# The tail of a ViT-tower kernel on one core: values, turns, scales and stores reordered, and two groups' outputs moved from VectorE to ScalarE and GpSimd

## The reference

```
lu, ru, ld, rd = four copies of x shifted by 4 pixels diagonally
c = concat(x, lu, ru, ld, rd)                    # 10 channels
c = (c - mean(c)) * rsqrt(var(c) + 1e-7) * gamma + beta    # per image
h = conv(c, W, stride 8) + b                     # 13 x 13 = 169 tokens of 128
h = concat(cls_tok, h)
n = layernorm(h);  q, k, v = n Wq^T, n Wk^T, n Wv^T
for t in tokens:  S = S + 0.01 * sum_b v[b,t] k[b,t]^T;  out[:, t] = S q[:, t]
h = h + out
result = h + ffn(layernorm(h))
```

## Time and profile before

| | |
|---|---|
| median of three runs | 229.32 us |
| the profiled execution | 229.03 us |
| its span | 227.2 us |
| TensorE busy | 198.8 us, 87% |
| GpSimd busy | 157.6 us, 69% |
| VectorE busy | 154.2 us, 68% |
| ScalarE busy | 112.1 us, 49% |
| granted TensorE clock, mean | 0.974 |

### The profile page before, as it was taken

One profiled execution on the slowest core, in us unless ns is written; L12 is line 12 of the kernel. 1 busy time (PEld: TensorE's weight loads), 2 busy tenths in 40 slices (PEclk: granted clock), 3 DMA queues, 4 the chain that ended last, 5 costly groups with the idle time before them and its releaser, 6 DMA issues.

```text
span 227.2 us, 4909 instructions
## 1 busy us (share of the span) xinstructions
PE 198.8 (87%) x1558; PEld 169.3 (75%) x1558; DVE 154.2 (68%) x760; ACT 112.1 (49%) x244; POOL 157.6 (69%) x124
## 2 busy tenths in 40 slices
PE   0299997899899999999999999999999999988500
PEld 0289886677688899888888888899888888876300
DVE  2658983351576786687777768579649866976971
ACT  6002211345334555565656585575566558475642
POOL 1049869899982899968999579669999235253130
PEclk9999999999999999999999999999999999999955
DMA  6999957913113005162053602012101211201434
GB/s 171 369 426 421 423 239 113 372 75 82 77 17 143 3 0 179 34 191 58 3 165 83 185 23 46 22 28 49 46 3 46 48 27 24 46 4 46 109 79 100
DMA packets 16543, 26.00 MB, mean 114 GB/s; under 512 B 1319, under 2 KB 13277, under 8 KB 16262
## 3 DMA queue, kind: packets, MB, share of 16 engines
q1 hardware_dynamic: 15836, 25.18, 34.7%
q10 hardware_dynamic: 682, 0.51, 0.7%
HBM read 19.77 MB, written 5.92 MB: 113 GB/s over the span
## 4 chain that ended last, share of the span: by engine, by line
PE 64%; DMA 12%; POOL 9%; DVE 8%; issue 2%; ACT 2%; SPq 0%; DVEq 0%; ACTq 0%; POOLq 0%
PE conv L462 29%; DMA rows<-x_windows 12%; PE vr_ps L504 11%; PE first_ps L514 9%; PE outs L531 9%; POOL scaled L382 7%; PE turn L494 4%; DVE scaled L382 2%; PE conv L468 2%; DVE images L819 1%; DVE state L790 1%; DVE state L798 1%; POOL g_low L1091 1%; DVE ln_stats L824 1%; PE conv L504 1%
## 5 line engine op out<-in xcount | busy, mean ns | idle before, releaser
L462 PE MATMUL conv<-scaled,wt 128*128 128x256 f32 (+3 forms) x460 | 116.0, 372 | 9.9 <-DMA wt<-weight 9.9
L382 POOL TENSOR_TENSOR scaled<-rows,gam 128x832 f32<-128x832 f32 x60 | 93.8, 1586 | 6.2 <-PE conv L462 4.2
L462 PEld LDWEIGHTS conv<-scaled,wt 128*128 128x128 f32 x460 | 77.1, 193 | 18.0 <-DMA wt<-weight 9.9
L666 ACT ACTIVATE values<-vr_ps,rstd 128x256 f32<-128x256 f32 x78 | 37.0, 475 | 64.8 <-PE vr_ps L504 54.5
L1101 POOL TENSOR_TENSOR rstd<-var,powers 128x8 f32<-128x8 f32 (+2 forms) x20 | 30.4, 1518 | 23.9 <-DVE var L810 23.9
L790 DVE TENSOR_TENSOR state<-first_ps,state 128x128 f32<-128x128 f32 x80 | 23.3, 291 | 31.5 <-PE first_ps L514 26.8
L674 ACT ACTIVATE images<-images,ln_shift,ln_gain 128x128 f32<-128x128 f32 x82 | 37.9, 484 | 4.8 <-DVE ln_shift L858 4.8
L504 PE MATMUL vr_ps<-w_high,g_low 128*128 128x256 f32 x80 | 32.0, 400 | 0.4 <-ACT values L666 0.4
L1091 POOL TENSOR_TENSOR g_low<-g_t,g_high 128x512 fp32r<-128x512 f32 x21 | 26.8, 1274 | 6.7 <-ACT g_high L653 5.9
L779 DVE BATCH_NORM_STATS2 ln_stats<-images 128x6 f32<-128x128 f32 x85 | 23.7, 284 | 6.7 <-ACT images L660 6.6
L798 DVE TENSOR_TENSOR state<-second_ps,state 128x128 f32<-128x128 f32 x80 | 22.6, 282 | 2.1 <-issue 0.3
(11 more groups left out here) (147 smaller groups left out, 236.6 us busy)
## 6 DMA issues: line engine op xcount, KB each, us to landing
rows<-x_windows SPq DMA_DIRECT2D x13, 864.0 KB, 5.6
out<-images SPq DMA_DIRECT2D x41, 128.0 KB, 2.4
images<-x_rows SPq DMA_DIRECT2D x3, 624.0 KB, 21.8
images<-x_rows SPq DMA_DIRECT2D x1, 1456.0 KB, 13.0
images<-x_rows SPq DMA_DIRECT2D x1, 1248.0 KB, 15.5
images<-x_rows SPq DMA_DIRECT2D x1, 832.0 KB, 19.6
small<-smalls SPq DMA_DIRECT2D x1, 512.0 KB, 8.6
terms<-parked SPq DMA_DIRECT2D x3, 168.0 KB
```

The lines of the kernel that those rows point to most:

```text
L382: return eng.tensor_tensor(scaled[:, s, at:at + N], window, gains, ALU.mult)
L462: last = pe.matmul(conv_ps[g % 2][:, at:at + n * B], wt[:, s], scaled[:, s, a % RING:a % RING + n], start=first, stop=(g < EARLY and s == ...
L666: act.activation(values[:, t % VALUE_SLOTS].rearrange("p a e -> p (a e)"), vr_bank(t)[:, 0:2 * E], ACT.Identity, scale=rho_of(t)).then_inc ...
```

## The change

- TensorE: `turn(LAST)` moves from the start of the tail into step 71, before `vr(75)`. `vr(82)` and `vr(83)` move ahead of `reads(18)`.
- ScalarE: `rows_out(20)` ahead of `values_out(76)`, `high(20)` behind it; finishing of tile 57 leaves step 70 and comes into the tail. New `out_copy(t)` for tiles 72 to 79: the output bank times rho into `h2`, laid between finished tiles.
- GpSimd: new `add_outs(g)` for groups 18 and 19: `h2 = h2 + h`, one 128x512 `tensor_tensor`.
- VectorE: `add_out` of tiles 72 to 79 goes; statistics of the tail's tiles are laid anew; `ln2_stats_of` of tiles 72 to 79 waits for GpSimd's sum. `ln2_affine(19)` comes before `ln2_moments(20)`.
- SyncE: tile 84 and the first half of group 20 leave in one DMA, behind the same waits.

```diff
@@ SyncE
-            sp.wait_ge(result_ready, LAST + 1)
-            sp.dma_start(out[:, PATCHES], tile_of(result, OUT_SLOTS, TILES - 1)[0:B]).then_inc(last_stored, 16)
             sp.wait_ge(result_ready, LAST + 2)
             sp.wait_ge(last_three_ready, 1)
-            sp.dma_start(out[:, bass.ds(1 + TOKENS * LAST, PER_GROUP, 2)],
-                         result[LAST % OUT_SLOTS].rearrange("p (k e) -> p k e", e=E)[0:B]).then_inc(last_stored, 16)
+            at = (H_SLOTS + H2_SLOTS + LAST % OUT_SLOTS) * width
+            sp.dma_start(out[:, bass.ds(1 + TOKENS * LAST, PER_GROUP + 1, 2)],
+                         spare[0:B, at:at + (PER_GROUP + 1) * E].rearrange("p (k e) -> p k e", e=E)).then_inc(last_stored, 16)
@@ TensorE, step
+                if t == TAIL - 1:
+                    turn(LAST)
                 if t + PER_GROUP >= 0:
                     vr(t + PER_GROUP)
@@ TensorE, tail
-                turn(LAST)
                 turn(LAST + 1)
...
                 vr(TAIL + 9)
+                vr(TAIL + 10)
+                vr(TAIL + 11)
                 pe.wait_ge(h2_ready, tile_no(TAIL - 1))
                 reads(g)
-                vr(TAIL + 10)
-                vr(TAIL + 11)
                 vr(TAIL + 12)
@@ ScalarE
+            def out_copy(t):
+                g, at = t // PER_GROUP, (t % PER_GROUP) * E
+                act.wait_ge(out_done, tile_no(tiles_of(g)[-1]))
+                act.activation(tile_of(h2, H2_SLOTS, t), out_bank(g)[:, at:at + E], ACT.Identity,
+                               scale=rho_of(t)).then_inc(out_scaled, 1)
...
-                    if finish_step(k) == t < TAIL - 1:
+                    if finish_step(k) == t < TAIL - 2:
                         finish_next(k)
@@ ScalarE, tail
+                rows_out(LAST)
                 values_out(TAIL + 4)
-                rows_out(LAST)
+                high(LAST)
                 rows_out(LAST + 1)
                 values_out(TAIL + 5)
-                high(LAST)
                 values_out(TAIL + 6)
                 values_out(TAIL + 7)
                 high(LAST + 1)
-                for t in range(TAIL - 14, TAIL - 11):
+                for t in range(TAIL - 15, TAIL - 11):
                     finish_next(t)
                 for t in LAST_TILES:
                     values_out(t)
-                for t in range(TAIL - 11, TAIL - 8):
+                finish_next(TAIL - 11)
+                for t in range(TAIL, TAIL + 4):
+                    out_copy(t)
+                for t in range(TAIL - 10, TAIL - 8):
                     finish_next(t)
+                for t in range(TAIL + 4, TAIL + 8):
+                    out_copy(t)
                 for t in range(TAIL - 8, LAST_TILES[0]):
                     finish_next(t)
@@ VectorE
             def ln2_stats_of(t):
-                dve.wait_ge(h2_ready, tile_no(t))
+                if TAIL <= t < LAST_TILES[0]:
+                    dve.wait_ge(pool_h2_ready, t // PER_GROUP - TAIL // PER_GROUP + 1)
+                else:
+                    dve.wait_ge(h2_ready, tile_no(t if t < TAIL else t - 2 * PER_GROUP))
@@ VectorE, tail, from the states of group 20 on
                 first_state(LAST_TILES[0])
-                add_out(TAIL)
                 second_state(LAST_TILES[0])
-                add_out(TAIL + 1)
                 first_state(LAST_TILES[1])
-                add_out(TAIL + 2)
                 second_state(LAST_TILES[1])
-                add_out(TAIL + 3)
+                ln2_affine(g - 1)
                 first_state(LAST_TILES[2])
-                ln2_affine(g - 1)
+                ln2_stats_of(TAIL)
                 second_state(LAST_TILES[2])
-                ln2_stats_of(TAIL)
+                ln2_stats_of(TAIL + 1)
                 first_state(LAST_TILES[3])
-                ln2_stats_of(TAIL + 1)
+                ln2_stats_of(TAIL + 2)
                 second_state(LAST_TILES[3])
-                ln2_stats_of(TAIL + 2)
+                ln2_stats_of(TAIL + 3)
                 first_state(LAST_TILES[4])
-                ln2_stats_of(TAIL + 3)
                 ln2_moments(g)
                 ln2_variance(g)
-                for t in tiles_of(g + 1):
+                group_stats(g + 1)
+                for t in LAST_TILES:
                     add_out(t)
-                group_stats(g + 1)
                 ln2_affine(g)
                 ln2_moments(g + 1)
                 ln2_variance(g + 1)
                 for t in LAST_TILES:
-                    add_out(t)
-                for t in LAST_TILES:
                     ln2_stats_of(t)
+                ln2_affine(g + 1)
                 ln2_moments(LAST)
                 ln2_variance(LAST)
-                ln2_affine(g + 1)
                 ln2_affine(LAST)
@@ GpSimd
+            def add_outs(g):
+
+                pool.wait_ge(out_scaled, tiles_of(g)[-1] - TAIL + 1)
+                pool.tensor_tensor(h2[g % H2_SLOTS], h2[g % H2_SLOTS], h[g % H_SLOTS], ALU.add).then_inc(pool_h2_ready, 1)
@@ GpSimd, tail
                 ln2_power(LAST - 3)
+                add_outs(TAIL // PER_GROUP)
+                add_outs(TAIL // PER_GROUP + 1)
                 ln2_power(LAST - 2)
```

More of the change, by code:

```diff
@@ L300, in tower @@
         last_three_ready = sem("last_three_ready")
+        out_scaled = sem("out_scaled")
+        pool_h2_ready = sem("pool_h2_ready")
         last_stored = sem("last_stored")
@@ L451, in _ @@
             sp.wait_ge(cls_stored, 16)
-            sp.wait_ge(last_stored, 48)
+            sp.wait_ge(last_stored, 32)
         @block.tensor
@@ L907, in tail @@
                 ln2_affine(g - 3)
+                ln1_stats_of(LAST_TILES[0])
                 first_state(TAIL)
-                ln1_stats_of(LAST_TILES[0])
+                ln1_stats_of(LAST_TILES[1])
                 second_state(TAIL)
-                ln1_stats_of(LAST_TILES[1])
+                ln1_stats_of(LAST_TILES[2])
                 first_state(TAIL + 1)
-                ln1_stats_of(LAST_TILES[2])
+                ln1_stats_of(LAST_TILES[3])
                 second_state(TAIL + 1)
-                ln1_stats_of(LAST_TILES[3])
+                ln1_stats_of(LAST_TILES[4])
                 first_state(TAIL + 2)
-                ln1_stats_of(LAST_TILES[4])
+                ln2_affine(g - 2)
                 second_state(TAIL + 2)
@@ L921, in tail @@
                 ln1_variance(LAST_TILES, last_var[:])
+                add_out(TAIL - 4)
                 second_state(TAIL + 3)
-                ln2_affine(g - 2)
-                add_out(TAIL - 4)
+                add_out(TAIL - 3)
                 first_state(TAIL + 4)
-                add_out(TAIL - 3)
+                add_out(TAIL - 2)
                 second_state(TAIL + 4)
-                add_out(TAIL - 2)
+                add_out(TAIL - 1)
                 first_state(TAIL + 5)
-                add_out(TAIL - 1)
+                ln2_stats_of(TAIL - 4)
                 second_state(TAIL + 5)
-                ln2_stats_of(TAIL - 4)
+                ln2_stats_of(TAIL - 3)
                 first_state(TAIL + 6)
-                ln2_stats_of(TAIL - 3)
+                ln2_stats_of(TAIL - 2)
                 second_state(TAIL + 6)
-                ln2_stats_of(TAIL - 2)
+                ln2_stats_of(TAIL - 1)
                 first_state(TAIL + 7)
-                ln2_stats_of(TAIL - 1)
+                ln2_moments(g - 1)
                 second_state(TAIL + 7)
-                ln2_moments(g - 1)
                 ln2_variance(g - 1)
                 first_state(LAST_TILES[0])
-                add_out(TAIL)
                 second_state(LAST_TILES[0])
-                add_out(TAIL + 1)
                 first_state(LAST_TILES[1])
-                add_out(TAIL + 2)
                 second_state(LAST_TILES[1])
-                add_out(TAIL + 3)
+                ln2_affine(g - 1)
                 first_state(LAST_TILES[2])
-                ln2_affine(g - 1)
+                ln2_stats_of(TAIL)
                 second_state(LAST_TILES[2])
-                ln2_stats_of(TAIL)
+                ln2_stats_of(TAIL + 1)
                 first_state(LAST_TILES[3])
-                ln2_stats_of(TAIL + 1)
+                ln2_stats_of(TAIL + 2)
                 second_state(LAST_TILES[3])
-                ln2_stats_of(TAIL + 2)
+                ln2_stats_of(TAIL + 3)
                 first_state(LAST_TILES[4])
-                ln2_stats_of(TAIL + 3)
                 ln2_moments(g)
                 ln2_variance(g)
-                for t in tiles_of(g + 1):
+                group_stats(g + 1)
+                for t in LAST_TILES:
                     add_out(t)
-                group_stats(g + 1)
                 ln2_affine(g)
```

## The result

| | us | ratio to before, 95% |
|---|---|---|
| before, median of 6 | 229.27 | |
| after, median of 6 | 227.38 | 0.992 (0.9909 to 0.993) |
| forecast | 227.1 (226.3 to 228.2) | |
| lowest of the versions tried (e10) | 226.21 | 0.9866 (0.9851 to 0.9881) |

The change gains 1.89; 2.25 was forecast. The mechanism is the forecast's up to the last issue; the landing behind it is not. The profiled execution took 227.42 with a span of 225.6. Ahead of every edit this trace already lies 0.27 later than the one of before (ScalarE's values(73) at 195.78 against 195.51), so 0.27 has to be taken off its positions when they are compared; behind the edits of part 1 it lies only 0.17 later (values at 201.16 against 200.99), which is what part 1 gains. The number in brackets is the position in the kernel before, as it stands.

What follows compares the result with a forecast made beforehand. VectorE was taken to set when the final store stream begins, and its bytes to decide the end. Work moved off VectorE and earlier products start the stream 2.25 earlier: 229.32 - 2.25 = 227.1, range 226.3 to 228.2.

Steps and rivals of the forecast that it cites:

- Bound: End of the kernel: set by when the final store stream begins, which VectorE's work sets; stream needs at least 2.8.
- Part 1: Group 20's transposes a step early, ScalarE's work ahead, finish tiles shifted: taken as 0, bounds -0.2 to +0.25.
- Part 2: vr(82), vr(83) ahead of reads(18) on TensorE: VectorE's first state of group 20 at 209.59 in place of 210.25.
- Rival E: Part 2 brings no earlier products; their gain is mostly eaten by the stall anyway: 227.3; chance 0.60 together with the forecast.
- Part 3: Outputs of groups 18 and 19 off VectorE: var(20) at 218.51 against 220.07, scale of group 19 2.25 earlier.
- the stall: VectorE's new wait of 0.42 for GpSimd at the statistics of tile 72, behind first_state(82).
- Rivals C and D: C: ScalarE and GpSimd hand over late, 227.7 or 227.9, chance 0.17. D: GpSimd's adds long enough to decide, 0.09.
- Part 4: Final stores: last issue 2.96 earlier, but the 544 KB stream ends at 223.95 against 226.2 and decides: 2.25.
- The prediction's own sign of being wrong: End of the kernel: forecast wrong if the last landing lay further than 3.2 behind the last issue.
- Rival B: The bytes don't bind; the end follows SyncE's last issue, 2.96 earlier: 226.4; chance 0.14.
- The rule weighed in part 3: GpSimd about 2x slower than VectorE on two-input elementwise work; by it 2.1 per group and about 227.9.

Runs made afterwards that it cites:

- e10: e7 with the second half of group 19's store issued by GpSimd in place of SyncE; 226.21.
- e12: e7 with ln2_affine(19) behind ln2_variance(20) again, as in the kernel before; 226.95.
- e3: The changed kernel with vr(82) and vr(83) behind reads(18) again; 227.60.
- e11: e1 with VectorE doing the outputs of groups 18 and 19 again and ln2_affine(19) behind ln2_variance(20); 228.44.
- e4: The kernel before with only vr(82) and vr(83) moved ahead of reads(18); 228.54.
- e7: e1 with finish(61) on ScalarE behind the four scalings of group 18 in place of ahead of them; 226.36.
- e1: The changed kernel with SyncE's last two DMAs apart as before (tile 84, then four tiles); 226.60.
- e8: e1 with ScalarE's last DMA storing one tile of the four, 96 KB left out; 226.70.
- e5: e1 with SyncE's two last DMAs in the other order, four tiles first, then tile 84; 226.74.
- e6: The changed kernel with a 128x512 copy on ScalarE before its last DMA, which did not wait for the copy; 227.44.
- e9: e6 with a wait, so that ScalarE's last DMA goes out only after the copy; 226.96.

## Why the prediction was right, and where not

- *Bound.* Right: VectorE sets when SyncE's row of issues begins, with group 19's tiles, and with the DMAs apart the end hangs on that row (e12).
- *Part 1.* 0 taken, 0.10 measured: equal starts in before and e3, and ScalarE's values at 200.99 and 200.89 behind the edits (e11 against e4 says 0.1 too, within the noise). I missed that the moved add_outs let the reads start earlier (e3).
- *Part 2.* 0.66 forecast at the first state; 0.64 in e4. In the changed kernel it is worth 0.22 beyond what part 1 and the moved add_outs bring. Rival E gave 0.2 for "a stall that is absorbed"; the number held, its reason didn't (e3).
- *Part 3.* Right in its terms but the stall: scalings 1.13 for four, adds 1.27 and 1.28, no wait for group 19. The stall was forecast as 0.42; the gap is 211.39 + 0.29 = 211.68 to 211.93, 0.25 by the profile, since the trace counts the state's whole 0.29 and I only the 0.20 to the next start (0.34 that way). Worth 0.24 (e7; 0.39 by the ratios). From the common start var(20) is at 218.31 for 218.51 and SyncE's row of issues begins at 219.63 for 219.83: 0.2 better than forecast, 0.10 of it part 1, the rest about the shorter stall. Rivals C and D fall.
- *Part 4, the step that failed.* "The stream ends later, so it decides." The bulk of the stream did end where it said, at 224.0 for 223.95, but a stream's end isn't a landing: I took the shift of the one for the shift of the other, and set a landing (223.8) against an end of bytes (223.95) to say which decides. Before, the last increment came 0.44 behind the last packet (226.31 to 226.75). After the change it came 1.1 behind the bulk: a last few packets of ScalarE's DMA end only at 224.35, and the last increment is 0.78 behind them, at 225.13. The prediction's own sign of being wrong, a last landing further than 3.2 behind the last issue, came true with 3.9. I treated the merge as an issue of 0.7 saved and nothing else; it also put ScalarE's bytes behind SyncE's, and costs 0.7 to 0.78 in this kernel (e1).
- *What sets the end when the DMAs are apart.* In e1 the row of issues begins 2.45 earlier than before and its last issue is 2.46 earlier, so the gain of 2.58 (0.9889) can't tell the bytes from the issues. e8 does: fewer bytes gain nothing. Rival B's view of the end, the last issue and 2.6 behind it, fits before, e1, e4, e5, e7, e8, e11 and e12. e10 shows that it ends soon: an issue 0.54 earlier gained 0.15.
- *Size.* Forecast 2.25, measured 1.89. The parts ahead of the stores gave 0.2 more than forecast, e1 measured 0.1 beyond that, and the landing took 0.7 back. From the common start the last increment moved from 226.75 to 224.86, which is the 1.89. Two errors of opposite sign: that the forecast of 227.1 lies within 0.3 of 227.38 is in part luck. The range would have held without it, since 226.60 lies in it too.

The rule weighed in part 3 (the Trainium skill, GPSIMD Engine Reference, section "Engine selection") speaks of 2x; the rows show 1.27 for a group against 1.05 on VectorE. The two are not the same work: VectorE's 1.05 also scales, which now takes ScalarE 1.13 for a group. The move won 1.84 all the same, since VectorE was the engine on the path and the two others had idle time there.

**Open.** Why the last increment is late. It came 0.78 to 0.85 behind the last packet in three kernels (after, e3, e6), in all of which SyncE's merged DMA was issued 0.03 to 0.04 behind ScalarE's and ScalarE's bytes came last; in the others it came 0.34 to 0.54 behind, in e9 too, where ScalarE's bytes are also last. The three have one thing in common: a packet of 8 KB of the instruction queue (q14 above) starts at 223.97, 223.90 and 224.02, takes 0.31, and the last packets of ScalarE's queue start just as it ends, at 224.27, 224.20 and 224.32; in e9 the like packet is over at 223.82, 0.5 ahead of the last one. It looks as if they stood behind it on one DMA engine; the trace doesn't name the engine of a packet, so this is argued and not shown, and it leaves the 0.8 behind the last packet without a cause. The Trainium skill (DMA: Bandwidth & Descriptors, section "Issuing engines are not separate DMA queues") has it that DMAs of ScalarE and SyncE run on the same 16 engines and interleave. Here two DMAs issued 0.04 apart hardly did: 300 packets of SyncE's queue passed between 222.5 and 223.4, and one of ScalarE's. Why SyncE's went first no run shows.

## What to carry to other kernels

Work moved to a slower engine pays when the engine it leaves is the one on the path: count the latency of the new chain against the place where its result is first wanted, and order the helper engine so that the chain comes first (e7). At the end of a kernel follow the row of DMA issues back to what starts it, and then ask of each queue when its last bytes move: a merged DMA saved an issue of 0.6, put the other queue's bytes last and left the kernel 0.7 slower. Where two DMAs raise one semaphore, look at the queues' packets before a late landing is put down to one of them.

## What the runs showed of the hardware that was not expected

- With 160 KB issued on SyncE's queue 0.03 to 0.04 behind 128 KB on ScalarE's, SyncE's bytes went first: 300 packets to 1 between 222.5 and 223.4 (after). The last landing was 3.8 to 3.9 behind SyncE's issue in three kernels (after, e3, e6).
- The last increment came 0.34 to 0.54 behind the last packet of the final stores in eleven kernels, and 0.78 to 0.85 behind it in those three.
- A DMA issued by ScalarE doesn't wait for the instruction ahead of it: in e6 it went out at 221.22 during a copy that ran from 221.05 to 221.65, and only a semaphore (e9) held it, to 221.59.
- A 128 KB store issued by GpSimd, 0.2 behind one of SyncE's, landed in 3.0, against 2.4 for SyncE's stores of that size (e10); one run, so the part of the neighbour is not told apart from the engine's.
- The stream of 512-byte rows, about 200 GB/s through most of it, ran at 300 to 338 GB/s in slices of 0.1 near its end (e1 and after), so a rate read from its middle is no ceiling.
